# Prelude of a fused two-layer attention and feed-forward kernel: the second tile is rounded and turned ahead of the context's last block, and the third tile's small scalars go to the end

## The reference

```python
x = x + _L0_xattn_ref(_layernorm(x), ctx_2048)            # stage a
x = x + _L0_ffn_ref(_layernorm(x), gate_w, up_w, down_w, gate_s, up_s, down_s)   # stage b
x = x + _L1_xattn_ref(_layernorm(x), ctx_2048, mask)      # stage c
x = x + _L1_ffn_ref(_layernorm(x), w_gate, w_up, w_down)  # stage d

def _L0_xattn_ref(x, weight):           # stage a: a product of two operands rounded to fp8 and back
    xq = quant_dequant_act_1x128(x)     # a scale for each row and each 128 columns
    wq = quant_dequant_weight_128x128(weight)   # a scale for each block of 128 x 128
    return jnp.einsum('emk,enk->emn', xq, wq)
```

## Time and profile before

| what | value |
|---|---|
| three timed runs | 724.7, 718.18, 723.27 us; median 723.27 |
| the profiled execution | 720.0 us, of which the span from first to last instruction is 718.2 us |
| mean granted clock of TensorE | 0.990 |
| busy: PE, DVE, ACT, POOL | 653.0, 589.5, 472.8, 368.5 us |
| the prelude, up to the first gate_up_b | 39.15 us |

### The profile page before, as it was taken

How to read it: one execution, slowest core, us unless ns; L and a number is a source line. 1 busy time by engine, 2 the same in 40 slices (tenths; PEclk the granted TensorE clock), 3 DMA queues, 4 the chain that set the end, 5 groups by cost and what they waited for, 6 DMA issues and landing times.

```text
span 718.2 us, 12556 instructions
## 1 busy us (share of the span) xinstructions
PE 653.0 (91%) x4086; PEld 375.3 (52%) x4086; DVE 589.5 (82%) x1386; ACT 472.8 (66%) x965; POOL 368.5 (51%) x291
## 2 busy tenths in 40 slices
PE   1788899999999999997999999997999999999996
PEld 0365566656666676752444444444444445444543
DVE  6889899999998888365877764788999899999874
ACT  3747467766776556375878833567787887778734
POOL 2023032323232413165767631079999998999970
PEclk9999899999999999998999999999999999999999
DMA  8971233333341322718999930445556655655611
GB/s 215 249 257 23 82 85 92 101 93 102 76 110 23 110 68 69 246 31 249 242 304 250 240 78 18 88 74 88 104 108 128 118 102 115 134 117 116 109 56 45
DMA packets 173131, 88.22 MB, mean 123 GB/s; under 512 B 150546, under 2 KB 152594, under 8 KB 172052
## 3 DMA queue, kind: packets, MB, share of 16 engines
q1 hardware_dynamic: 167188, 71.94, 43.4%
q10 hardware_dynamic: 3408, 11.27, 4.8%
q0 software_dynamic: 2480, 4.33, 3.4%
HBM read 51.20 MB, written 4.19 MB: 77 GB/s over the span
## 4 chain that ended last, share of the span: by engine, by line
PE 48%; DVE 22%; ACT 10%; issue 7%; POOL 6%; DMA 5%; SPq 1%; POOLq 0%; ACTq 0%; DVEq 0%
PE ps L1840 10%; PE ps L1687 8%; PE ps L1764 7%; PE ps L1782 7%; PE ps L1702 5%; DMA arena<-arena 4%; PE ps L1820 3%; DVE X L1114 3%; PE ps L1912 2%; POOL arena L537 2%; POOL arena L538 2%; DVE arena L1204 2%; ACT arena L881 2%; DVE y_sm L1511 2%; PE ps L1880 2%
## 5 line engine op out<-in xcount | busy, mean ns | idle before, releaser
L1687 PE MATMUL ps<-arena 128*128 128x256 f16 x1408 | 162.7, 275 | 11.0 <-DVE arena L1204 5.7
L1687 PEld LDWEIGHTS ps<-arena 128*128 128x128 f16 x1408 | 137.0, 99 | 38.0 <-DVE arena L1204 9.1
L465 POOL TENSOR_TENSOR arena<-arena 128x256 f16<-128x256 f32 x88 | 57.7, 675 | 183.1 <-ACT arena L640 182.6
L1840 PE MATMUL ps<-arena 128*128 128x512 bf16 x512 | 118.3, 380 | 8.8 <-ACT arena L852 7.6
L537 POOL TENSOR_TENSOR arena<-arena 128x1024 f32<-128x1024 f32 x44 | 103.7, 2358 | 43.7 <-DVE arena L1485 40.2
L538 POOL TENSOR_TENSOR arena<-arena 128x1024 f32<-128x1024 f32 x44 | 104.0, 2364 | 0.0
L1840 PEld LDWEIGHTS ps<-arena 128*128 128x128 bf16 x512 | 47.7, 98 | 68.4 <-DVE arena L1477 10.2
L1702 PE MATMUL ps<-arena 128*128 128x512 f16 x352 | 78.6, 379 | 3.6 <-POOL arena L465 3.5
L633 ACT ACTIVATE arena<-ps,gs 128x256 f32<-128x256 f32 x88 | 40.7, 466 | 53.3 <-PE ps L1687 53.2
L1764 PE MATMUL ps<-arena 128*128 128x512 f16 x256 | 60.4, 391 | 5.5 <-DMA arena<-arena 5.5
L1912 PE MATMUL ps<-arena 128*128 128x512 bf16 x256 | 59.8, 379 | 1.5 <-ACT arena L925 1.5
(11 more groups left out here) (160 smaller groups left out, 1208.7 us busy)
## 6 DMA issues: line engine op xcount, KB each, us to landing
arena<-in_ctx_t SPq DMA_DIRECT2D x7, 1024.0 KB, 6.1
arena<-in_wg_t SPq DMA_DIRECT2D x16, 256.0 KB, 3.9
arena<-in_wu_t SPq DMA_DIRECT2D x16, 256.0 KB, 4.4
arena<-in_wd_t SPq DMA_DIRECT2D x16, 256.0 KB, 5.0
arena<-in_ctx_n SPq DMA_DIRECT2D x4, 1024.0 KB, 9.7
arena<-in_wu_t ACTq DMA_DIRECT2D x4, 1024.0 KB, 5.7
arena<-in_wd_t ACTq DMA_DIRECT2D x4, 1024.0 KB, 5.8
out_x<-X SPq DMA_DIRECT2D x16, 256.0 KB, 2.5
```

Source lines behind the costliest of these rows:

```text
L465: nc.gpsimd.tensor_tensor(hl[:, c, at:at + 2 * P], b_h[n % 4], hh[:, c, at:at + 2 * P], ALU.subtract).then_inc(b_hl_r, 1)
L1687: last = M(bank(n % 2)[:, 2 * P * i:2 * P * i + 2 * P], W[:, b, c * P:c * P + P], part[:, b, at:at + 2 * P], start=(b == 0 and part is xhT ...
L1840: last = M(bank(2 * (n % 2) + i), d_qT[u][:, b, :], W[:, b, D * n:D * n + D], start=(b == 0), stop=(b == KD - 1))
```

## The change

Three orders change; no operation is added or removed.

- On DVE, the rounding of tile 1 (a_grids(1), a_rounding(1)) moves ahead of the rounding of the context's block 3. The norm of tile 2 keeps its place, but its a_smalls_of moves from there to behind first_low(1), the last piece of the prelude.
- On ACT, context_back(0, 3) moves behind a_back(1) and a_evac(1), and a_scale(2) moves behind b_evac(1).
- On PE, first_product(0) is split: three blocks, then a_turn(1), then the fourth block, then first_product(1).

```diff
@@ ACT
             context_back(0, 2)
-            context_back(0, 3)
             a_back(1)
             a_evac(1)
+            context_back(0, 3)
             act.wait_ge(ds_ps, 1)
             nc.scalar.activation(ds_bc[:, :], bank(7), ACT.Copy).then_inc(ds_r, 1)
-            a_scale(2)
             act.wait_ge(row_in, 64)
             nc.scalar.activation(b_sil[0][:, 0:1], gs[:, 0:1], ACT.Silu)
             b_evac(0)
             b_evac(1)
+            a_scale(2)
@@ DVE
             context_rounding(0, 2)
+            a_grids(1)
+            a_rounding(1)
             context_grid(0, 3)
             context_rounding(0, 3)
-            a_grids(1)
-            a_rounding(1)
...
             a_stats(2)
             a_residual(0)
             b_stats(0)
-            a_norm(2)
+            a_normal(2)
             b_norm(0)
             a_residual(1)
             b_stats(1)
             first_low(0)
             b_norm(1)
             first_low(1)
+            a_smalls_of(2)
@@ PE
-            def first_product(j):
-                pe.wait_ge(a_xT_r, j + 1)
-                wait(pe, a_add, j)
-                for b in range(KD):
+            def first_product(j, first=0, end=KD):
+                if first == 0:
+                    pe.wait_ge(a_xT_r, j + 1)
+                    wait(pe, a_add, j)
+                for b in range(first, end):
...
-                last.then_inc(a_mm, 1)
+                if end == KD:
+                    last.then_inc(a_mm, 1)
...
             a_turn(0)
-            first_product(0)
+            first_product(0, 0, KD - 1)
             a_turn(1)
+            first_product(0, KD - 1, KD)
             first_product(1)
```

## The result

| | before | changed |
|---|---|---|
| median of 19 timed executions each | 720.29 us | 725.71 us |
| lowest to highest | 718.07 to 724.7 | 719.66 to 731.35 |
| ratio, changed to before | 1.0059, 95% interval 1.0036 to 1.0082 | |
| profiled execution, span | 718.2 us | 724.4 us |
| mean granted clock | 0.990 | 0.985 |

The change makes the kernel slower by 0.59%, which is 4.2 us with an interval of 2.6 to 5.9. The forecast was +3.2 us. Disturbed executions are left out of every ratio: the one of 731.35 here, and single ones of 1374 us and more further on.

A forecast was written before the change was run, and what follows sets the result against it. The prediction took the prelude to be bound by a chain of ACT and PE waits, then by DVE from 39.04 us. 2.07 + 1.12 = +3.19 us, added to a mean of 721.5, gave 724.7 us, range 719.5 to 730.5.

The forecast's parts named there:

- the new wait: Prelude: context_back(0, 3) waits on ACT behind a_evac(1), so PE idles 1.9 us before tile 0's fourth block.
- +2.07 at the second product: Prelude, PE: the second product starts 2.07 us later, after the fourth block and a_residual(0), which uses the same bank 5.
- The smalls: End of prelude, DVE: a_smalls_of(2), four instructions between first_low(1) and context_max(1), delays all that follows on DVE by 1.12 us.
- a delay of DVE at 39 us goes through group 0 whole: DVE has no idle time with a releaser from 39.04 to 74.9 us, so the whole delay reaches the next groups.
- A: Rival: PE's clock falls in the prelude's new idle time; +6.6 us, 728.1 us; chance 0.20, 0.05 of it with two stretches.
- between 1.8 and 2.4 us of idleness: PE: the length of idle time at which the granted clock starts to fall; the new 1.9 us is close to it.
- 3.4: PE: work lost in us to one fall of the clock, ahead of group 1 or in the second product's eight passes.
- B: Rival: not slower, as the clock's fall ahead of group 1 stays away and returns 3.4 us; -0.2 us, 721.3 us; chance 0.08.
- C: Rival: tile 1's second product starts at the time of before, leaving only +1.1 us, 722.6 us; chance 0.12.
- the central case: The forecast itself, prelude delays with no added clock loss: +3.19 us, 724.7 us, chance 0.60.

The follow-up runs named there:

- again: The changed kernel itself measured once more, with no edit: 1.0051 of the kernel before, +3.7 us.
- orders only: The changed kernel with only tile 2's pieces (a_smalls_of(2), a_scale(2)) put back in their old places: 1.0072 of the kernel before, +5.2 us.
- other bank: The changed kernel with tile 1's product in bank 1 and not bank 5: 1.0073 of the kernel before.
- warm: The changed kernel with 24 products that nothing reads in PE's idle time ahead of a_turn(0): 1.0026 of the kernel before.
- the smalls alone: The kernel before with only a_smalls_of(2) moved behind first_low(1) and a_scale(2) behind b_evac(1): 1.0003 of the kernel before.
- the kernel with the fills: The changed kernel with products that nothing reads, 7 behind a_turn(1) and 2 behind tile 0's fourth block: 1.0038 of the kernel before, +2.7 us.
- the kernel without the stretch: The kernel before with 11 products that nothing reads in PE's idle time ahead of group 1: 0.9982 of the kernel before, -1.3 us.

## Why the prediction was right, and where it was not

**The place and the size of the new wait: right.** PE was idle for 1.85 us (1.9 forecast), and for 0.87 for a_residual(0) (0.75). Moving one line on ACT took the first idle time away, which shows its cause. The +2.07 at the second product was +1.66 in the execution where the clock held, with quicker first passes, and 2.1 to 2.2 with those as before. Wherever the smalls were moved, the delay of the first b_hidden is the sum of three rows: the later start of the second product, its extra length, and 1.11 for the smalls (2.90 + 3.04 + 1.11 = 7.05 of 7.06 in the changed kernel, 2.57 + 2.33 + 1.11 = 6.01 of 6.02 in its repetition).

**The smalls: right in price, too high in the whole.** 1.11 us on DVE (1.12 forecast), handed on to group 1 in full. The step that failed is "a delay of DVE at 39 us goes through group 0 whole, and the next groups start from what group 0 leaves": true up to the start of group 1, but group 1 itself is not of fixed length. Before, a stretch of lower clock made DVE wait 0.92 and 0.26 us in it; in the changed kernel the stretch took less of the work, DVE did not wait, and the group was 1.1 us shorter. The forecast had looked for slack on DVE in group 0 and had none for the clock in group 1.

**The clock: a rival, and it was the usual case.** A was given 0.20. Of the five profiles with the 1.85 us unfilled (changed, again, orders only, other bank, warm) the clock fell in four. The 18 timed executions of the changed kernel that the ratio rests on agree: four had a mean clock of 0.993 to 0.995 and took 719.7 to 721.2 us, the others 0.985 to 0.991 and 723.3 to 729.3. The failed step is the decisive point "between 1.8 and 2.4 us of idleness", taken from one fall and from gaps elsewhere between long runs of work. That one fall was also read wrongly: a window of 1 us that reads 0.64 was at the full clock for 0.28 of it, so the fall came at 79.28, after 2.0 us of idleness and not 2.4. And there is no such point in the traces. Ahead of group 1 PE is idle for 3.1 us in these kernels, and by the same reading the fall came 2.0 us into this in the kernel before, 2.6 in the orders alone, and in the changed kernel and the smalls alone only when PE had been at work again for 0.3 and 1.0 us. Behind the 1.85 us it came 0.4 to 0.8 us into the work that followed (other bank, again, warm) or in the 0.87 us after it (changed), and with the same two idle times it did not come in the orders alone.

The price of one fall was nearer 3.0 than 3.4: 3.04 us in the second product of the changed kernel, 3.1 by the comparison with the fills. The rest of the 7.06 is no fall: 2.01 + 1.11 are about what the orders and the smalls cost, and 0.8 come from the first passes, which were slow for longer in this execution (5.49 us for six), as they also were in the kernel with the fills (also 5.49), where the clock held later. What the Trainium skill says in "TensorE: Matmul & The Clock Gate", Part 1, that the number of matmuls at the lower clock differs between executions of one kernel, agrees with the six first passes: 4.57 to 5.49 us without any edit that could reach them.

**B and C.** B's premise, that the slow stretch ahead of group 1 is worth 3.4 us, was wrong twice. The 0.36 us of the window 79 to 80 and the first 0.37 us of the next were idle time, in which a lower clock costs nothing: PE was at work at half only from 80.37 to about 86.1, which is 2.9 us of lost work. Of these the group loses 1.5, and the kernel without the stretch gained 1.3, because DVE sets the pace there. C is excluded: the second product never started at the time of before in the changed order (10.65 at the earliest, against 8.99).

**The sum.** The forecast +3.2 stood against +4.2 measured (2.6 to 5.9), and 724.7 against a median of 725.71. Two errors of opposite sign lie in this: 1.1 us given back in group 1 (not foreseen), and about 3 us lost to the clock in most executions (foreseen in one of five). By the parts, as an estimate, 3.1 - 1.1 + 14/18 of 3.0 = 4.3. But the timed executions are not spread as this says. The four with the higher clock took 720.6 us in the mean, which is the mean of the kernel before (720.7), and the other fourteen 726.1, or 5.4 more. Almost none took what the central case said. Four executions are few, and picking them by their clock favours quick ones, so whether the fixed 2 us are really there in the whole is open; what is shown is that nearly all of the loss is in the executions with the lower mean clock, as in A. So the number was near largely by luck. The waits on ACT, PE and DVE were right as the profiles show them; the weights of the clock cases and what the later groups do with a delay were not.

## What to carry to other kernels

On an engine that works its list in order, a step that waits for another engine holds up all that stand behind it: before moving one forward, ask what is behind it and who needs that, here the fourth block's rescaling behind a copy that waited for a turn. Work that is hidden in a wait (the smalls, a_residual(0)) becomes a cost when it is moved out of the wait or the wait is moved. And an added wait on PE may have to be priced twice, once for itself and once for the clock, of which the second was the larger here (3.0 against 2.1 us); a difference at one place is then to be followed through the later stages, since the clock can give back or take as much as the edit did.

## What the runs showed of the hardware that I had not expected

- The granted clock fell after short gaps with short work between them: 1.85 us, two passes, 0.87 us (changed kernel), and 1.16 and 0.99 us around four transposes (warm). It did not always: with the first of these patterns it held in the profile of the orders alone. A gap of 1.87 us between 32 passes of 128x256 and 32 more, in group 0 of the changed kernel (49.5 to 51.4 us), did not lower it.
- The first passes run at the lower level (0.85 us apart) while the granted clock reads 1.00 in the windows view (25 to 28 us); pass durations are the better witness at the start of an execution.
- A whole kernel with a mean granted clock of 0.998 was 0.7% slower than one with 0.990: with PE kept busy in stage c, a wait that seems to be one for transfers came two tiles later, and a new fall behind it; the cause of the whole loss is open.
- The load of the Silu table takes 1.28 us, and the next ACT instruction starts 1.30 after its start (32.81 and 34.11 in the changed kernel). The Trainium skill, "ScalarE: Activation LUTs", section on what ACT_TABLE_LOAD costs, adds a drain of about 1.4 us to it, which does not show here.
